# Layer normalisation of a small language-model tower: centred values kept in SBUF, variances of four pairs in one PSUM tile, deviations spread by row tiles

## The chip, the cores and the metric

One core of one Trainium2 chip runs the whole program in a single launch. The metric is the device time of that launch in microseconds (us), lower is better.

## The reference

The tower takes 32 sequences of 512 tokens, turns them into features of width 64 and passes them through four residual blocks. Each block first normalises its input without gain or bias:

```python
def _layernorm(x, axis=-1, eps=1e-05):
    m = jnp.mean(x, axis=axis, keepdims=True)
    v = jnp.var(x, axis=axis, keepdims=True)
    return (x - m) / jnp.sqrt(v + eps)

h = _L0_tok_ref(x, ...)                       # spectral tokenizer
h = h + _L0_attn_ref(_layernorm(h), ...)      # neighbourhood attention
h = h + _L0_ffn_ref(_layernorm(h), ...)       # mixture of experts, top 2 of 8
h = h + _L1_attn_ref(_layernorm(h), ...)      # decayed linear attention
h = h + _L1_ffn_ref(_layernorm(h), ...)       # soft mixture; its router takes the mean
                                              # of the normalised rows over the batch
```

## The kernel before

The residual stream `s.h` and the normalised values `s.z` live in SBUF for the whole program, as rows of 128 partitions by 512 columns in float32. One row is a pair of sequences: partitions 0 to 63 are the features of the first, 64 to 127 those of the second, columns are tokens. There are NP = 16 pairs. The program is a string of stages, each a block of its own with five instruction streams (TensorE, ScalarE, VectorE, GpSimd, SyncE) that meet at its end; only then does the next stage begin. `layer_norm` is such a stage and stands four times in the string, as ln0 to ln3, ahead of the four residual blocks. No stage prefetches anything for the next.

Inside `layer_norm`, for each pair: TensorE multiplies `s.h` by `center` (identity minus the mean over 64 features) into one of four PSUM tiles `cen` (L703). ScalarE squares it into SBUF, `sq` (L720). TensorE multiplies `sq` by `mean64`, a 128 by 128 matrix of two 64 by 64 blocks, so that every partition of `var` (one of four PSUM tiles) holds the variance of its own sequence (L708). ScalarE takes the logarithm of the variance plus eps (L725) and the exponential of minus half of it (L730), the reciprocal deviation `rstd`. VectorE multiplies `cen`, from PSUM, by `rstd` into `s.z` (L740). In ln3 GpSimd also adds every row of `s.z` to `s.feat` as it comes (L761); in ln0 it clears and fills two window buffers.

The order on each engine is written out by hand: `staggered` and `unrolled` take stages with a lead, and at step n each engine issues, in the order of the list, stage by stage, the work of pair n + lead. TensorE issues the variance of pair n + 2 and the centre of pair n + 4; ScalarE the root of n, the logarithm of n + 1, the squares of n + 3. `staggered` puts the middle of the work in a hardware loop of four pairs, `unrolled` writes all out. Engines wait for each other by counting semaphores; `done(n)` is the count at which pair n is finished, and a negative n is satisfied from the start.

Of the kernel before, what the change touches and what calls it, by code (L numbers as in the profile page):

```python
# [21 lines left out]
F32 = mybir.dt.float32  # L22
# [27 lines left out]
def window_start(t):  # L50
# [2 lines left out]

CONST_PARTS = [("ident", 128), ("dft", 4 * 2 * NF), ("shift", T), ("center", 128), ("mean64", 128), ("mean128", 128),
               ("decay", 128), ("chunk_q", 128), ("chunk_k", 1), ("winmask", 4 * WIN), ("headmask", HL), ("vmask", 18), ("rank", NE),
               ("pick", EP * 128), ("moe_b2", 2)]
CONST_AT = {}
# [8 lines left out]
def constants():  # L68
    c = {}
    c["ident"] = np.eye(128)  # L70
    block = np.kron(np.eye(2), np.full((D, D), 1.0 / D))
    c["center"] = np.eye(128) - block
    c["mean64"] = block
    c["mean128"] = np.full((128, 128), 1.0 / HID)
    t = np.arange(T)[:, None] * np.arange(NF)[None, :] % T * (2 * np.pi / T)
    dft = np.concatenate([np.cos(t), -np.sin(t)], 1)
    c["dft"] = dft.reshape(4, 128, 2 * NF).transpose(1, 0, 2).reshape(128, -1)

    step = np.float32(2.0 * np.pi / T)
    shift = (step * np.arange(T, dtype=np.float32)[None, :]) * np.arange(NF, dtype=np.float32)[:, None]  # L80
    shift = shift.astype(np.float64)
    c["shift"] = np.concatenate([np.cos(shift), np.sin(shift)] * 2, 0)
    k, q = np.arange(128)[:, None], np.arange(128)[None, :]
    c["decay"] = np.where(q >= k, np.power(float(np.float32(ALPHA)), np.maximum(q - k, 0)), 0.0) / np.sqrt(D)
    c["chunk_q"] = np.broadcast_to(np.power(float(np.float32(ALPHA)), q + 1) / np.sqrt(D), (128, 128))
    c["chunk_k"] = np.power(float(np.float32(ALPHA)), 127 - k)
    mask = np.full((4, QT, WIN), NEG)
    for kind, tile in enumerate((0, 1, 2, NT - 1)):
        for r in range(QT):
            first = min(max(tile * QT + r - KW // 2, 0), TG - KW) - window_start(tile)  # L90
            mask[kind, r, first:first + KW] = 0.0
    c["winmask"] = np.tile(mask.transpose(1, 0, 2).reshape(QT, -1), (4, 1))
    c["headmask"] = np.kron(np.ones((4, 1)), np.kron(np.eye(HL), np.ones((DH, 1))))
    v = np.zeros((128, 18))
    v[:WIN, 0:8] = v[WIN:2 * WIN, 8:16] = 1.0
    v[:WIN, 16] = v[WIN:2 * WIN, 17] = 1.0
    c["vmask"] = v
    c["rank"] = np.broadcast_to(np.arange(NE, 0, -1), (128, NE))
    pick = np.zeros((4, ROUTES, EP, 128))
    for e in range(NE):  # L100
        pick[:, [e, NE + e], e // 2, (e % 2) * 64:(e % 2) * 64 + 64] = 1.0
    c["pick"] = pick.reshape(128, -1)
    parts = np.zeros((4, ROUTES, 2))
    parts[:, 0:2 * NE, 0] = parts[:, 2 * NE:3 * NE, 1] = 1.0
    c["moe_b2"] = parts.reshape(128, 2)
    return np.ascontiguousarray(np.concatenate([c[n] for n, _ in CONST_PARTS], 1).astype(np.float32))

# [80 lines left out]
def const(s, name, rows=128):  # L188
    at, n = CONST_AT[name]
    return s.const[0:rows, at:at + n]  # L190
# [248 lines left out]
def done(n):  # L439

    return n + (1 + CREDITS)


def give_credits(eng, *semaphores):
    for sem in semaphores:
        eng.sem_inc(sem, CREDITS)  # L446


def row(t, n):

    return t[:, bass.ds(n, 1), :].rearrange("p a b -> p (a b)")
# [16 lines left out]
def staggered(eng, count, unroll, *stages):  # L468


    most = max(lead for lead, _ in stages)
    for n in range(-most, 0):
        for lead, stage in stages:
            if n + lead >= 0:
                stage(Step(0, n + lead, unroll))
    last = max(1, -(-most // unroll))
    turns = count // unroll - last
    with eng.Fori(0, turns) as turn:
        for k in range(unroll):
            for lead, stage in stages:  # L480
                stage(Step(turn, k + lead, unroll))
    for k in range(last * unroll):
        for lead, stage in stages:
            if k + lead < last * unroll:
                stage(Step(turns, k + lead, unroll))


def unrolled(count, unroll, *stages):


    most = max(lead for lead, _ in stages)
    for n in range(-most, count):
        for lead, stage in stages:
            if 0 <= n + lead < count:
                stage(Step((n + lead) // unroll, (n + lead) % unroll, unroll))
# [188 lines left out]
def layer_norm(nc, s, tag, features=False, windows=None):  # L684


    with ExitStack() as ctx:
        def sb(name):
            return [ctx.enter_context(nc.sbuf_tensor(f"{tag}_{name}{k}", [128, T], F32)) for k in range(4)]

        sq, ln, rstd = sb("sq"), sb("ln"), sb("rstd")
        cen, var = [[ctx.enter_context(nc.psum_tensor(f"{tag}_{x}{k}", [128, T], F32)) for k in range(4)] for x in ("cen", "var")]
        s_cen, s_sq, s_var, s_ln, s_rstd, s_z, s_feat = [ctx.enter_context(nc.semaphore(f"{tag}_s_{x}"))
                                                         for x in ("cen", "sq", "var", "ln", "rstd", "z", "feat")]
        block = ctx.enter_context(nc.Block())

        @block.tensor
        def _(te):
            give_credits(te, s_cen, s_var)

            def centre(at):
                te.wait_ge(s_z, done(at.n - 4))
                nc.tensor.matmul(cen[at.k][:], const(s, "center"), row(s.h, at.n), start=True, stop=True).then_inc(s_cen, 1)  # L703

            def variance(at):
                te.wait_ge(s_sq, done(at.n))
                te.wait_ge(s_ln, done(at.n - 4))
                nc.tensor.matmul(var[at.k][:], const(s, "mean64"), sq[at.k][:], start=True, stop=True).then_inc(s_var, 1)  # L708

            staggered(nc.tensor, NP, 4, (2, variance), (4, centre))  # L710

        @block.scalar
        def _(sc):
            sc.preload_act_table_set("natural_log_exp_and_others")
            give_credits(sc, s_sq, s_ln, s_rstd)

            def squares(at):
                sc.wait_ge(s_cen, done(at.n))
                sc.wait_ge(s_var, done(at.n - 4))
                nc.scalar.activation(sq[at.k][:], cen[at.k][:], ACT.Square).then_inc(s_sq, 1)  # L720

            def logarithm(at):
                sc.wait_ge(s_var, done(at.n))
                sc.wait_ge(s_rstd, done(at.n - 4))
                nc.scalar.activation(ln[at.k][:], var[at.k][:], ACT.Ln, bias=s.eps[:]).then_inc(s_ln, 1)  # L725

            def root(at):
                sc.wait_ge(s_ln, done(at.n))
                sc.wait_ge(s_z, done(at.n - 4))
                nc.scalar.activation(rstd[at.k][:], ln[at.k][:], ACT.Exp, scale=-0.5).then_inc(s_rstd, 1)  # L730

            staggered(nc.scalar, NP, 4, (0, root), (1, logarithm), (3, squares))

        @block.vector
        def _(ve):
            give_credits(ve, s_z)

            def normalise(at):
                ve.wait_ge(s_rstd, done(at.n))
                nc.vector.tensor_tensor(row(s.z, at.n), cen[at.k][:], rstd[at.k][:], ALU.mult).then_inc(s_z, 1)  # L740

            staggered(nc.vector, NP, 4, (0, normalise))

        @block.gpsimd
        def _(pool):
            if windows:
                for t in windows:
                    nc.gpsimd.memset(t[:], 0.0).then_inc(s_feat, 1)
                pool.wait_ge(s_feat, 2)
                for t in windows:  # L750
                    sums = t[:, :, :, :, 16:18].rearrange("p a b c d -> p (a b c) d")
                    nc.gpsimd.tensor_tensor(sums, sums, const(s, "vmask")[:, 16:18].unsqueeze(1).broadcast_to([128, 2 * NT * NH, 2]), ALU.add)\
                        .then_inc(s_feat, 1)
                pool.wait_ge(s_feat, 4)
            if features:
                give_credits(pool, s_feat)

                def add(at):
                    pool.wait_ge(s_z, done(at.n))
                    pool.wait_ge(s_feat, done(at.n - 1))  # L760
                    nc.gpsimd.tensor_tensor(s.feat[:], s.feat[:], row(s.z, at.n), ALU.add).then_inc(s_feat, 1)  # L761

                staggered(nc.gpsimd, NP, 4, (0, add))
# [897 lines left out]
```

## Time and profile before

| what | value |
|---|---|
| median of 3 runs | 1034.17 us |
| lowest, highest | 1033.28, 1040.14 us |
| the profiled execution, its own time | 1035.37 us |
| its span, first to last instruction | 1033.6 us |
| TensorE busy | 931.0 us, 90% |
| ScalarE busy | 596.1 us, 58% |
| VectorE busy | 581.5 us, 56% |
| GpSimd busy | 174.6 us, 17% |

The profile is of one execution. Its span leaves out 1.8 us of that execution's own time, and the own time is 1.2 us above the median of the runs. Busy time of TensorE is the union of its matmuls, whose ends are modelled; weight loads are counted apart (PEld). A float32 matmul appears as two weight loads and two matmul records.

### The profile page before, as it was taken

To read this page: it belongs to the slowest core of one execution; us is meant where nothing else is said; L and a number is where in the kernel's file an instruction comes from. 1 tells how busy PE (TensorE), PEld (TensorE's weight loads), DVE (VectorE), ACT (ScalarE), POOL (GpSimd) and SP (SyncE) were. 2 spreads that over 40 slices of the span, in tenths; PEclk is the share of its full clock that TensorE was granted. 3 is DMA by queue.
4 is the path that set the end of the run, shared out by engine and by line. 5 is a ranking of instruction groups with operands and counts; after the bars stand their busy time and mean duration, and the time that the engine had idled before them with its cause. 6 is when DMAs were issued, how large, how long until landed. Compare 5 with 4: busy or idle time off the path is not lost. (4 is left out here: it accounts for less than half of the span.)

```text
span 1033.6 us, 29479 instructions
## 1 busy us (share of the span) xinstructions
PE 931.0 (90%) x12388; PEld 449.2 (43%) x12388; DVE 581.5 (56%) x797; ACT 596.1 (58%) x822; POOL 174.6 (17%) x209
## 2 busy tenths in 40 slices
PE   3977969999999998937999999979999689999998
PEld 2331437767777675412222222347774422222222
DVE  3655237767777675366675755348873234444443
ACT  2998857777677775834444444742227445555553
POOL 1214121322313130061000000001114370000000
PEclk9998989999999999967999999989999899999999
DMA  2210000000000000000000000012110011111110
GB/s 54 28 28 1 0 1 5 4 4 4 4 4 5 4 4 3 1 1 1 1 1 1 1 1 1 1 42 53 42 32 1 0 36 56 43 42 42 41 42 31
DMA packets 27512, 17.15 MB, mean 17 GB/s; under 512 B 18753, under 2 KB 23010, under 8 KB 27394
## 3 DMA queue, kind: packets, MB, share of 16 engines
q1 hardware_dynamic: 26626, 14.16, 5.9%
q8 instruction: 97, 1.59, 0.6%
q10 hardware_dynamic: 768, 1.23, 0.3%
q14 instruction: 21, 0.17, 0.1%
HBM read 2.80 MB, written 4.19 MB: 7 GB/s over the span
## 5 line engine op out<-in xcount | busy, mean ns | idle before, releaser
L1585 DVE SCALAR_TENSOR_TENSOR se_a<-se_p,cols,z 128x1024 f32<-128x1024 f32 x64 | 82.2, 1284 | 119.1 <-PE se_p L1528 119.1
L1563 ACT ACTIVATE se_a<-se_p,cols 128x512 f32<-128x512 f32 x128 | 92.5, 773 | 79.9 <-PE se_p L1518 79.9
L1141 ACT ACTIVATE me_g<-me_p,cols 128x1024 f32<-128x1024 f32 x64 | 71.3, 1114 | 83.6 <-PE me_p L1095 83.6
L1232 DVE TENSOR_TENSOR me_gw<-me_pc,me_g 128x1024 f32<-128x1024 f32 x64 | 78.3, 1224 | 62.6 <-PE me_pc L1107 56.6
L991 DVE TENSOR_REDUCE na_rowmax<-na_ps 128x16 f32<-128x1024 f32 x64 | 78.0, 1218 | 60.9 <-PE na_ps L887 60.9
L801 POOL TENSOR_TENSOR z<-na_k,const 128x512 f32<-128x512 f32 x64 | 64.5, 1040 | 210.3 <-ACT na_k L940 210.3
L740 DVE TENSOR_TENSOR z<-ln_cen,ln_rstd 128x512 f32 (+1 forms) x64 | 44.2, 691 | 85.3 <-ACT ln_rstd L730 85.3
L994 DVE TENSOR_TENSOR na_e<-na_ps,na_rowmax 128x1024 f32<-128x1024 f32 x64 | 78.3, 1224 | 2.2
L703 PE MATMUL ln_cen<-h,const 128*128 (+1 forms) x128 | 69.7, 634 | 6.2 <-DVEq L446 6.2
L1518 PE MATMUL se_p<-z,f_w 64*64 64x512 f32 x256 | 70.5, 623 | 4.0 <-DMA se_zswap<-z 4.0
L896 PE MATMUL na_pt<-const,na_e 128*128 128x128 f32 x512 | 69.2, 278 | 3.3 <-ACT na_et L970 1.7
L1095 PE MATMUL me_p<-z,moe_w 64*64 64x512 f32 x512 | 70.7, 623 | 0.0
L970 ACT ACTIVATE na_et<-na_pt 128x1024 f32<-128x1024 f32 x64 | 65.4, 1023 | 8.7 <-PE na_pt L896 7.8
L1518 PE MATMUL se_p<-se_zswap,f_w 64*64 64x512 f32 x256 | 69.7, 623 | 0.0
L1538 PE MATMUL se_py<-se_a,f_wo 128*64 128x512 f32 x256 | 69.1, 618 | 0.4 <-DVE se_a L1585 0.4
L1117 PE MATMUL me_py<-me_gw,moe_w 128*64 128x512 f32 x256 | 69.0, 618 | 0.4 <-DVE me_gw L1232 0.4
L963 ACT ACTIVATE na_e<-na_e 128x1024 f32<-128x1024 f32 x64 | 67.4, 1054 | 1.5 <-DVE na_e L994 1.1
L1528 PE MATMUL se_p<-se_a,f_w 64*64 64x512 f32 x512 | 67.2, 595 | 1.1 <-DVE se_a L1585 1.1
L708 PE MATMUL ln_var<-ln_sq,const 128*128 128x512 f32 x128 | 65.8, 601 | 0.0
L896 PEld LDWEIGHTS na_pt<-const,na_e 128*128 128x128 f32 x512 | 56.2, 141 | 14.8 <-issue 12.0
L957 ACT ACTIVATE na_v<-na_pm 64x512 f32<-64x512 f32 x64 | 38.5, 602 | 29.0 <-PE na_pm L847 28.6
L913 PE MATMUL na_po<-na_v,na_et 128*32 128x18 f32 x4096 | 49.2, 187 | 4.4 <-issue 3.1
(222 smaller groups left out, 1539.1 us busy)
## 6 DMA issues: line engine op xcount, KB each, us to landing
da_zswap<-z SPq DMA_DIRECT2D x32, 128.0 KB, 2.3
se_zswap<-z SPq DMA_DIRECT2D x32, 128.0 KB, 2.4
out<-se_rows SPq DMA_DIRECT2D x16, 256.0 KB, 2.1
const<-in_const ACTq DMA_DIRECT2D x1, 720.5 KB, 5.0
f_w<-in_L_ffn_W SPq DMA_DIRECT2D x4, 128.0 KB
const<-in_const ACTq DMA_DIRECT2D x1, 448.0 KB, 3.9
moe_w<-in_L_ffn_w SPq DMA_DIRECT2D x2, 128.0 KB
raw<-in_L_ffn_b SPq DMA_DIRECT2D x12, 2.0 KB
```

The source lines that it names most:

```text
L703: nc.tensor.matmul(cen[at.k][:], const(s, "center"), row(s.h, at.n), start=True, stop=True).then_inc(s_cen, 1)
L896: mm = nc.tensor.transpose(p_t[:, c, :], e[b][:, 2 * c:2 * c + 2, :].rearrange("p h w -> p (h w)"), const(s, "ident"))
L991: nc.vector.tensor_reduce(rowmax[b][:], scored, AX, ALU.max).then_inc(s_max, 1)
L994: nc.vector.tensor_tensor(e[b][:], scored, rowmax[b][:].unsqueeze(2).broadcast_to([128, GROUPS, WIN]), ALU.subtract).then_inc(s_diff, 1)
L1095: mm = nc.tensor.matmul(p_1[half[e2], b, :], s.moe_w1[half[b], 2 * ep + e2, :], row(s.z, at.of(4))[half[b], :], start=True, stop=True, ski ...
L1117: mm = nc.tensor.matmul(p_y[slot][half[b], :], s.moe_w2[:, ep, :], gw[at.k % 2][:, b, :], start=False, stop=(ep == EP - 1), skip_group_che ...
L1141: nc.scalar.activation(g[at.k % 2][:], p_1[:], ACT.Gelu, bias=col(s, "moe_b1", ep)).then_inc(s_g, 1)
L1232: nc.vector.tensor_tensor(gw[at.k % 2][:], p_c[:], g[at.k % 2][:], ALU.mult).then_inc(s_gw, 1)
L1518: mm = nc.tensor.matmul(p_1[at.k % 2][half[b], e2, :], s.f1_w1[half[e2], 2 * ep + e2, :], z[half[e2], :], start=True, stop=True, skip_grou ...
L1538: mm = nc.tensor.matmul(p_y[half[b], :], s.f1_wo[:, ep, :], a2[at.k % 2][:, b, :], start=(ep == 0), stop=(ep == EP - 1), skip_group_check= ...
L1563: ins = nc.scalar.activation(a1[at.k % 2][:, e2, :], p_1[at.k % 2][:, e2, :], ACT.Relu, scale=col(s, "f1_g1", 2 * ep + e2), bias=col(s, "f ...
L1585: nc.vector.scalar_tensor_tensor(out=a2[at.k % 2][:], in0=p_2[:], scalar=col(s, "f1_be2", ep), in1=s.f1_w[:, ep, :].unsqueeze(1).broadcast ...
```

## The change

All of it is in `layer_norm` and in two constants.

- VectorE copies each `cen` tile to `s.z` (`move`) and later multiplies it there in place (`normalise`). ScalarE squares from `s.z`. `cen` has three tiles in place of four, and a centre matmul waits for the move of the pair three before it.
- `mean64` shrinks from 128 to 32 columns, of which two are not zero. The variances of four pairs go to the four 32-partition quarters of a single tile `var`, by four matmuls of 128 rows by 32 columns of the array.
- ScalarE takes one logarithm and one exponential for four pairs, the second in place on the first.
- TensorE spreads each quarter of `rstd` over 128 partitions with a new constant `select` (32 rows by 128 columns of the array), into one of four tiles `wide`. There is one set of `wide`.
- All three engines run `unrolled`, with leads of 9, 4 and 3 pairs on TensorE (centre, variance, spread), 7 and 4 on ScalarE (squares, deviations), 8 and 0 on VectorE (move, normalise). GpSimd's part is as it was.

```diff
-    c["mean64"] = block
+    c["mean64"] = np.kron(np.eye(2, 32), np.full((D, 1), 1.0 / D))
+    c["select"] = np.tile(np.kron(np.eye(32, 2), np.ones((1, D))), (4, 1))
...
-        sq, ln, rstd = sb("sq"), sb("ln"), sb("rstd")
-        cen, var = [[... [128, T], F32)) for k in range(4)] for x in ("cen", "var")]
+        sq, rstd = sb("sq", 8), sb("rstd", 2)
+        cen, var, wide = ps("cen", 3), ps("var", 1)[0], ps("wide", 4)
...
             def centre(at):
-                te.wait_ge(s_z, done(at.n - 4))
-                nc.tensor.matmul(cen[at.k][:], const(s, "center"), row(s.h, at.n), start=True, stop=True).then_inc(s_cen, 1)
+                te.wait_ge(s_moved, done(at.n - 3))
+                nc.tensor.matmul(cen[at.n % 3][:], const(s, "center"), row(s.h, at.n), start=True, stop=True).then_inc(s_cen, 1)
 
             def variance(at):
-                te.wait_ge(s_sq, done(at.n))
-                te.wait_ge(s_ln, done(at.n - 4))
-                nc.tensor.matmul(var[at.k][:], const(s, "mean64"), sq[at.k][:], start=True, stop=True).then_inc(s_var, 1)
-
-            staggered(nc.tensor, NP, 4, (2, variance), (4, centre))
+                if at.k == 3:
+                    te.wait_ge(s_sq, done(at.n))
+                    te.wait_ge(s_ln, done(at.of(4) - 1))
+                    for j in range(4):
+                        mm = nc.tensor.matmul(var[32 * j:32 * j + 32, :], const(s, "mean64"), sq[(at.n - 3 + j) % 8][:], start=True, stop=True,
+                                              skip_group_check=True)
+                    mm.then_inc(s_var, 1)
+
+            def spread(at):
+                if at.k == 3:
+                    q = at.of(4)
+                    te.wait_ge(s_rstd, done(q))
+                    te.wait_ge(s_z, done(4 * q - 1))
+                    for j in range(4):
+                        r = slice(32 * j, 32 * j + 32)
+                        mm = nc.tensor.matmul(wide[j][:], const(s, "select")[r, :], rstd[q % 2][r, :], start=True, stop=True, skip_group_check=True)
+                    mm.then_inc(s_wide, 1)
+
+            unrolled(NP, 4, (9, centre), (4, variance), (3, spread))
...
             def squares(at):
+                sc.wait_ge(s_moved, done(at.n))
+                sc.wait_ge(s_var, done((at.n - 8) // 4))
+                nc.scalar.activation(sq[at.n % 8][:], row(s.z, at.n), ACT.Square).then_inc(s_sq, 1)
+
+            def deviations(at):
+                if at.k == 3:
+                    q = at.of(4)
+                    sc.wait_ge(s_var, done(q))
+                    sc.wait_ge(s_wide, done(q - 2))
+                    nc.scalar.activation(rstd[q % 2][:], var[:], ACT.Ln, bias=s.eps[:]).then_inc(s_ln, 1)
+                    sc.wait_ge(s_ln, done(q))
+                    nc.scalar.activation(rstd[q % 2][:], rstd[q % 2][:], ACT.Exp, scale=-0.5).then_inc(s_rstd, 1)
+
+            unrolled(NP, 4, (7, squares), (4, deviations))
...
+            def move(at):
+                ve.wait_ge(s_cen, done(at.n))
+                nc.vector.tensor_copy(row(s.z, at.n), cen[at.n % 3][:]).then_inc(s_moved, 1)
 
             def normalise(at):
-                ve.wait_ge(s_rstd, done(at.n))
-                nc.vector.tensor_tensor(row(s.z, at.n), cen[at.k][:], rstd[at.k][:], ALU.mult).then_inc(s_z, 1)
-
-            staggered(nc.vector, NP, 4, (0, normalise))
+                ve.wait_ge(s_wide, done(at.of(4)))
+                ve.wait_ge(s_sq, done(at.n))
+                nc.vector.tensor_tensor(row(s.z, at.n), wide[at.k][:], row(s.z, at.n), ALU.mult).then_inc(s_z, 1)
+
+            unrolled(NP, 4, (8, move), (0, normalise))
```

## Rows read from the trace of the kernel before

**Rows 1.** The four layer_norm stages, ln0 to ln3: busy time per stretch.

```profile
core 0: us, PE busy (x) PEld busy (x) DVE busy (x) ACT busy (x) POOL busy (x), PEclk, DMA share, GB/s
103.60:135.70 32.10, 29.50 (x64) 12.51 (x64) 11.06 (x16) 28.22 (x49) 4.85 (x4) 0.95 0.00 0
...
779.80:812.00 32.20, 27.90 (x64) 11.85 (x64) 11.06 (x16) 28.19 (x49) 20.29 (x16) 0.98 0.00 1
```

**Rows 2.** Timeline of ln0, mid-stage: start us, duration us, engine, line.

```profile
112.27 1.02 PE L708 MATMUL ln_var<-ln_sq,const 128*128 128x512 f32 x2
...
113.12 1.02 PE L703 MATMUL ln_cen<-h,const 128*128 x2
...
113.98 1.02 PE L708 MATMUL ln_var<-ln_sq,const 128*128 128x512 f32 x2
...
114.18 0.60 ACT L720 ACTIVATE ln_sq<-ln_cen 128x512 f32<-128x512 f32 x1
...
114.68 0.62 ACT L730 ACTIVATE ln_rstd<-ln_ln 128x512 f32<-128x512 f32 x1
```

**Rows 3.** Timeline of ln1: its first centre, first variance, first normalise, last deviation.

```profile
414.72 3.59 PE L703 MATMUL ln_cen<-h,const 128*128 128x512 f32 x4 [1.41 <-DVEq L446]
...
418.14 1.02 PE L708 MATMUL ln_var<-ln_sq,const 128*128 128x512 f32 x2
...
421.32 0.69 DVE L740 TENSOR_TENSOR z<-ln_cen,ln_rstd 128x512 f32 x1 [7.22 <-ACT ln_rstd L730]
...
444.95 0.67 ACT L725 ACTIVATE ln_ln<-ln_var,eps 128x512 f32<-128x512 f32 x1
...
445.65 0.63 ACT L730 ACTIVATE ln_rstd<-ln_ln 128x512 f32<-128x512 f32 x1
446.31 0.69 DVE L740 TENSOR_TENSOR z<-ln_cen,ln_rstd 128x512 f32<-128x512 f32 x1 [0.55 <-ACT ln_rstd L730]
```

**Rows 4.** Timeline of ln3: first centre, last additions, last normalise, next stage.

```profile
779.81 1.95 PE L703 MATMUL ln_cen<-h,const 128*128 128x512 f32 x4 [1.35 <-DVEq L446]
...
807.85 4.08 POOL L761 TENSOR_TENSOR feat<-feat,z 128x512 f32<-128x512 f32 x3 [0.45 <-DVE z L740]
...
809.55 0.69 DVE L740 TENSOR_TENSOR z<-ln_cen,ln_rstd 128x512 f32<-128x512 f32 x1 [0.55 <-ACT ln_rstd L730]
...
812.27 2.04 PE L1424 MATMUL sr_p<-f_wr,feat 128*128 128x128 f32 x8 [4.57 <-PEq L687]
```

**Rows 5.** Timeline of the soft experts: three sets of tiled matmuls.

```profile
850.65 0.64 PE L1518 MATMUL se_p<-z,f_w 64*64 64x512 f32 x1
...
851.55 1.04 PE L1528 MATMUL se_p<-se_a,f_w 64*64 64x512 f32 x8
...
852.52 1.08 PE L1538 MATMUL se_py<-se_a,f_wo 128*64 128x512 f32 x4
...
853.53 0.64 PE L1518 MATMUL se_p<-z,f_w 64*64 64x512 f32 x1
```

**Rows 6.** Windows of L1072 alone (router, four 128*32 tiles), at full clock.

```profile
500.00:520.00 20.00, 1.07 (x8) 0.16 (x8) 1.00 0.00 1
```

**Rows 7.** Groups of matmuls by form: tiles of 32 rows.

```profile
L887 PE MATMUL na_ps<-z,na_q 32*32 32x256 f32 x2048 | 51.9, 390 | 0.2 <-issue 0.2
...
L1107 PE MATMUL me_pc<-me_ct,pick_r 32*128 32x512 f32 x128 | 32.1, 495 | 0.7 <-DVE me_gw L1232 0.4
```

**Rows 8.** Timeline of VectorE in the decayed attention: two reads of PSUM in a row.

```profile
689.33 0.69 DVE L1375 TENSOR_TENSOR da_v<-da_pv,a_bvk 128x512 f32<-128x512 f32 x1 [7.56 <-PE da_pv L1316]
...
689.94 0.74 DVE L1376 SCALAR_TENSOR_TENSOR da_kd<-da_pv,const,a_bvk 128x512 f32<-128x512 f32 x1
```

**Rows 9.** Copies on VectorE by form, from PSUM and from SBUF.

```profile
L1176 DVE COPY me_logits<-me_pr 128x256 f32<-128x256 f32 x4 | 1.7, 417 | 4.6 <-PE me_pr L1077 4.6
L1221 DVE COPY me_ctin<-me_high 128x256 f32<-128x256 f32 x4 | 1.2, 294 | 0.1
```

**Rows 10.** GpSimd additions by form, in the experts and in ln3.

```profile
L1059 POOL TENSOR_TENSOR h<-h,z 128x512 f32<-128x512 f32 x16 | 21.5, 1379 | 0.0
L761 POOL TENSOR_TENSOR feat<-feat,z 128x512 f32<-128x512 f32 x16 | 20.3, 1268 | 18.4 <-DVE z L740 18.1
```

More of the change, by code:

```diff
@@ L52, in window_start @@
     return min(max(t * QT - KW // 2, 0), TG - WIN)
-CONST_PARTS = [("ident", 128), ("dft", 4 * 2 * NF), ("shift", T), ("center", 128), ("mean64", 128), ("mean128", 128),
+CONST_PARTS = [("ident", 128), ("dft", 4 * 2 * NF), ("shift", T), ("center", 128), ("mean64", 32), ("select", 128), ("mean128", 128),
                ("decay", 128), ("chunk_q", 128), ("chunk_k", 1), ("winmask", 4 * WIN), ("headmask", HL), ("vmask", 18), ("rank", NE),
@@ L687, in layer_norm, with sb, ps @@
     with ExitStack() as ctx:
-        def sb(name):
-            return [ctx.enter_context(nc.sbuf_tensor(f"{tag}_{name}{k}", [128, T], F32)) for k in range(4)]
-        sq, ln, rstd = sb("sq"), sb("ln"), sb("rstd")
-        cen, var = [[ctx.enter_context(nc.psum_tensor(f"{tag}_{x}{k}", [128, T], F32)) for k in range(4)] for x in ("cen", "var")]
-        s_cen, s_sq, s_var, s_ln, s_rstd, s_z, s_feat = [ctx.enter_context(nc.semaphore(f"{tag}_s_{x}"))
-                                                         for x in ("cen", "sq", "var", "ln", "rstd", "z", "feat")]
+        def sb(name, n):
+            return [ctx.enter_context(nc.sbuf_tensor(f"{tag}_{name}{k}", [128, T], F32)) for k in range(n)]
+        def ps(name, n):
+            return [ctx.enter_context(nc.psum_tensor(f"{tag}_{name}{k}", [128, T], F32)) for k in range(n)]
+        sq, rstd = sb("sq", 8), sb("rstd", 2)
+        cen, var, wide = ps("cen", 3), ps("var", 1)[0], ps("wide", 4)
+        s_cen, s_sq, s_moved, s_var, s_ln, s_rstd, s_wide, s_z, s_feat = [ctx.enter_context(nc.semaphore(f"{tag}_s_{x}"))
+                                                                         for x in ("cen", "sq", "moved", "var", "ln", "rstd", "wide", "z", "feat")]
         block = ctx.enter_context(nc.Block())
@@ L698, in _ @@
         def _(te):
-            give_credits(te, s_cen, s_var)
+            give_credits(te, s_cen, s_var, s_wide)
             def centre(at):
-                te.wait_ge(s_z, done(at.n - 4))
-                nc.tensor.matmul(cen[at.k][:], const(s, "center"), row(s.h, at.n), start=True, stop=True).then_inc(s_cen, 1)
+                te.wait_ge(s_moved, done(at.n - 3))
+                nc.tensor.matmul(cen[at.n % 3][:], const(s, "center"), row(s.h, at.n), start=True, stop=True).then_inc(s_cen, 1)
             def variance(at):
-                te.wait_ge(s_sq, done(at.n))
-                te.wait_ge(s_ln, done(at.n - 4))
-                nc.tensor.matmul(var[at.k][:], const(s, "mean64"), sq[at.k][:], start=True, stop=True).then_inc(s_var, 1)
-            staggered(nc.tensor, NP, 4, (2, variance), (4, centre))
+                if at.k == 3:
[15 more added lines that the diff above has]
+            unrolled(NP, 4, (9, centre), (4, variance), (3, spread))
         @block.scalar
@@ L717, in squares @@
             def squares(at):
[L718 to L732, printed above, removed]
+                sc.wait_ge(s_moved, done(at.n))
[10 more added lines that the diff above has]
+            unrolled(NP, 4, (7, squares), (4, deviations))
         @block.vector
         def _(ve):
-            give_credits(ve, s_z)
+            give_credits(ve, s_moved, s_z)
+            def move(at):
+                ve.wait_ge(s_cen, done(at.n))
+                nc.vector.tensor_copy(row(s.z, at.n), cen[at.n % 3][:]).then_inc(s_moved, 1)
             def normalise(at):
-                ve.wait_ge(s_rstd, done(at.n))
-                nc.vector.tensor_tensor(row(s.z, at.n), cen[at.k][:], rstd[at.k][:], ALU.mult).then_inc(s_z, 1)
-            staggered(nc.vector, NP, 4, (0, normalise))
+                ve.wait_ge(s_wide, done(at.of(4)))
+                ve.wait_ge(s_sq, done(at.n))
+                nc.vector.tensor_tensor(row(s.z, at.n), wide[at.k][:], row(s.z, at.n), ALU.mult).then_inc(s_z, 1)
+            unrolled(NP, 4, (8, move), (0, normalise))
         @block.gpsimd
```

## The prediction

> **What bounds the kernel now.** I read the page's busy times first (TensorE 90%), then the busy time of the four normalisation stages by windows, then their timelines, because stages don't overlap and only these four change. Each stage is 32.1 to 32.3 us long and TensorE is busy in 28 to 29.5 us of it, ScalarE in 28.2, VectorE in 11.1 [rows 1]. The timeline shows what sets the pace: centre, variance and centre start 0.85 and 0.86 us apart [rows 2], so a pair costs TensorE 2 x 0.858 = 1.716 us and four pairs 6.86 us; nothing in between is idle. ScalarE, three operations a pair, starts them 0.5 us apart at the closest (square to exponential, 114.18 to 114.68 [rows 2]) and keeps up, just. ln1 runs from its first centre at 414.72 to the end of its last normalise at 446.31 + 0.69 = 447.00: 32.28 us. Its first two centres take until 418.14, 1.71 us each, twice 0.858: that is the clock at 1.2 in place of 2.4 GHz after the idle of the stage's start [rows 3]. ln3 starts at the full clock and its z is ready at 810.24, but what ends it is GpSimd: three additions in 4.08 us, 1.36 us from one to the next, up to 811.93, and the router's first matmul starts at 812.27 [rows 4]. So ln3 is 32.12 us long, and its end hangs on additions of which 16 need 21.8 us.
>
> **The price of a set of tiles.** The trace has no set like the new two, but near ones. In the soft experts a set of four 64*64 matmuls is followed after 0.90 us by another of the same form, and sets followed by another form take 0.97 and 1.01 us [rows 5]. So a set of tiles that covers the array costs 0.90 us against 0.858 for one full matmul, and a change of form some 0.12 us more. The router's set of four 128*32 tiles is the form of the new variance: 1.07 us from start to the end of its results [rows 6], in line with 1.04 and 1.08 in rows 5. The Trainium skill ("TensorEngine Tiling (Array Packing)", Key Properties) says that changing the tiling mode drains TensorE; the trace agrees, and prices the drain at about 0.12 us. I take 1.02 us for variance and spread alike, plus 0.12 where a centre stands before one.
>
> The spread is the less certain. Its four tiles of 32 rows each write all 128 partitions of a bank of their own, in float32. For it speaks L887: 32 float32 matmuls of 256 columns in tiles of 32*32, all four row groups, in 51.9 / 32 = 1.62 us a step, where row groups taken one after another would need 8 x 0.43 = 3.4 us [rows 7]. L1107 has two 32*128 tiles side by side, 32.1 / 64 = 0.50 us for both [rows 7]. Bounds: 0.90 us (rows 5) and 4 x 0.858 = 3.43 us, no overlap; I take the low end, since both nearest rows overlap. The Trainium skill ("TensorE: Matmul & The Clock Gate", Measured speedup vs the span model) gives a speedup of 3.07 for four row tiles of 512 columns; by that the set would take 3.43 / 3.07 = 1.12 us (an estimate from that page), and the sum would be about 1.5 us longer.
>
> **The other parts.** Two PSUM-reading operations on VectorE start 0.61 us apart, and the first takes 0.69 [rows 8]. A copy of 256 columns from PSUM takes 0.417 us and from SBUF 0.294 [rows 9], so the move has no short form; between 0.417 and twice that for 512 columns, I take the 0.69 of an operation of that size in rows 8, 0.61 from start to start and 0.74 until a waiter goes on. Eight of them, for four pairs, are 4.9 us: under what TensorE needs, however VectorE is now close behind. ScalarE falls from twelve operations to six for four pairs and is free. Logarithm to exponential is 0.70 us and exponential to the waiting engine 0.66 [rows 3]. `const` grows by 32 columns, loaded stages before: nothing. The written-out loops replace hardware loops; I cost that at nothing, as the other stages are written out and TensorE runs without gaps in them [rows 5].
>
> **What replaces the bound.** By count, four pairs now take TensorE 4 x 0.858 + 2 x 1.02 + 0.12 = 5.6 us, 1.3 less than 6.86. But its queue is in order: variance of group g, one centre, spread of group g, three centres. From the start of a variance to the start of its spread lie 1.07 (matmuls) + 0.08 (hand-over) + 0.70 + 0.66 = 2.51 us, and the one centre fills only up to 1.02 + 0.86 = 1.88. TensorE stands 0.6 us in each group, with centres queued behind the wait. The period is 0.12 + 2.51 + 1.02 + 3 x 0.858 = 6.22 us, a gain of 0.64, not 1.3. VectorE's loop (seven operations from one group's first normalise, 6 x 0.61 + 0.74, then the next spread 1.15) is 5.55 us and fits below.
>
> Head: nine centres must go out before the first variance, where before it followed the second. In ln1 the first two end at 3.42, the ninth at 9.43; variance 9.55, spread 12.06, first normalise 1.15 later at 13.21 (before: 6.60 [rows 3]). Then the second group's normalise at 19.43, and the last centre ends at 21.02. The third group: variance 21.14, but its logarithm stands behind the square of pair 14, whose move starts at 21.26 and ends by 22.0, and 0.5 after that square's start it starts, at 22.5; spread 23.86, normalise 25.01. The fourth: variance 24.88, but the single set of `wide` is free only when pair 11 is done, 25.01 + 3 x 0.61 + 0.74 = 27.6; spread 27.6, four normalises from 28.75, the end at 31.27. Against 32.28 ln1 gains 1.0 us; ln0 and ln2 start as cold, so 3.0 us for the three.
>
> ln3 is warm, so everything is 1.70 us earlier: normalises of the four groups begin at 11.51, 17.73, 23.31 and 27.05. The first addition starts at 12.25 and each group's four take 5.44 us: 12.25 to 17.69, 18.47 to 23.91, 24.05 to 29.49, then without a pause to 34.93. Before it was 32.12: a loss of 2.8 us, since GpSimd gets its first row 5 us later than before and has no speed to make it up. If additions are slowed by VectorE's doubled work (1.38 us in place of 1.27, as L1059 in the experts [rows 10]), 16 x 0.11 = 1.8 us more.
>
> **Sum.** -3.0 + 2.8 = -0.2 us against the profiled execution's own 1035.37, so 1035.2; that run was 1.2 above the median, so 1034.0. A kernel whose runs spread from 1033 to 1040 can't tell less than 1% from no change. The forecast's own range is 1029 to 1039: 0.12 us up or down for each of 16 groups' two sets, and the additions' 1.8.
>
> **Rivals.**
> - *The spread's tiles go two at a time.* Each set then takes 2 x 0.858 + 0.12 = 1.84, 0.82 more, and all of it lies on the path: four times in ln0 to ln2, 9.8 us, and in ln3 the last group's additions begin about 2.5 us later. 1034.0 + 12.3 = 1046, slower by 1.2%; at full serial order some 1070. It decides once a set costs over 1.65 us. Against it: L887 and L1107. For it: no row has four full-width float32 outputs at once. 0.10 (with the serial end).
> - *The count decides.* If the spread found its deviations ready, TensorE would set the pace and ln0 to ln2 would end with it: 1.7 + 16 x 0.858 + 8 x 1.02, then 1.15 + 3 x 0.61 + 0.69, is 27.3 us, 4.0 less than above for each of three stages: 1034.0 - 12 = 1022, faster by 1.2%. For it: TensorE is what bounds these stages. Against it: the order of the queue and 1.36 us of ScalarE in series. 0.10.
> - *VectorE takes over.* If its operations start 0.75 us apart and not 0.61, its loop is 6 x 0.75 + 0.88 (0.14 longer as well) + 1.15 = 6.5 us, over 6.22, and the tails grow by 0.6 us: 1034.0 + 4 = 1038. 0.08, inside the range. The Trainium skill names this outcome ("TensorEngine Tiling (Array Packing)", PSUM Bottleneck: the copy out of PSUM may become the bottleneck after tiling); here rows 8 speak against it.
> - *The change doesn't do what it says*: float32 tiles don't overlap at all, the serial end above.
>
> The forecast has 0.72, with VectorE's case 0.80. Range 1025 to 1043, which leaves out 0.2 at the two ends. Faster by over 1%: 0.12; within 1%: 0.75; slower by over 1%: 0.13, the last with a little for slow hand-overs that I haven't found.
>
> **What the changed profile would show.** Right: the variance and spread sets 1.0 to 1.1 us each; TensorE idle about 0.6 us before each spread, released by ScalarE; first normalises near 13.2 us after the first centre (11.5 in ln3), groups 6.2 us apart; ln0 to ln2 about 31.3 us long; GpSimd's additions without a gap from the second half of ln3 on, ending 35 us after the first centre. Wrong: a spread of 1.6 us or more; normalises under 6 us apart; a third clock-bound centre in the head; additions that end with the last normalise.

## The result, and the profile after

The changed kernel takes 1039.72 us (median of 19 runs, 1036.72 to 1047.66) against 1035.26 for the kernel before in as many runs: ratio 1.005, 95% interval 1.0034 to 1.0066. It is slower by about 5 us (3.5 to 6.8 by the interval). The forecast was 1034.0, no change, in a range of 1025 to 1043: the time lies in the range, but the loss is real and was not forecast. The profiled execution took 1038.47, its span is 1036.7 us.

Stage by stage, from the first matmul of one to the first of the next, read from the timelines of both traces (us):

```
                      before   after
up to ln0              103.6   105.5   not touched by the change
ln0                     33.7    31.7
neighbourhood attn.    277.4   276.9
ln1                     33.5    31.2
experts                201.5   201.5
ln2                     35.5    35.2
decayed attention       94.6    94.7
ln3                     32.5    36.8
router                  18.0    19.2
soft experts           203.2   204.2
```

Before anything is read into ln0 and ln1, the clock has to be taken out. After, they happened to start at 2.4 GHz and ln2 at 1.2; before, all three started at 1.2. Windows of the four changed stages (columns as in [rows 1]):

```profile
105.40:135.50 30.10, 23.31 (x96) 7.57 (x96) 20.35 (x32) 15.57 (x25) 4.73 (x4) 0.99 0.00 0
414.00:444.00 30.00, 23.30 (x96) 7.53 (x96) 20.35 (x32) 15.50 (x25) 0.00 (x0) 0.96 0.00 1
646.60:678.40 31.80, 25.00 (x96) 8.21 (x96) 20.34 (x32) 15.59 (x25) 0.00 (x0) 0.93 0.00 1
776.50:813.00 36.50, 23.30 (x96) 7.57 (x96) 20.35 (x32) 15.56 (x25) 20.30 (x16) 0.92 0.00 0
```

TensorE's busy time fell from some 28 to 29.5 us to 23.3 or 25.0 and ScalarE's from 28.2 to 15.6, as the change meant. VectorE's rose from 11.1 to 20.4. The stages did not shorten with TensorE. From first centre to last normalise they take 29.98 us from a warm clock (ln0, ln1, ln3) and 31.67 from a cold one (ln2); before, 30.43 (ln3) and 32.04 (ln0, ln2). Like for like, such a stage gains 0.4 us. ln1 before was the longest, 32.28 from a cold clock; it took 30.75 from a warm one where the old stage ran in a later kernel (e2), and the changed one took 31.61 from a cold clock in another (e3). So ln1 gains 0.7 us, and ln0 to ln2 together gain 1.5.

TensorE in ln3, after, shows why (timeline: start us, duration us; in brackets the idle before it and what ended it):

```profile
776.55 7.96 PE L707 MATMUL ln_cen<-h,const 128*128 128x512 f32 x18 [1.50 <-DVEq L447]
784.44 1.06 PE L714 MATMUL ln_var<-ln_sq,const 128*32 128x512 f32 x8
785.44 1.12 PE L707 MATMUL ln_cen<-h,const 128*128 128x512 f32 x2
786.98 1.14 PE L725 MATMUL ln_wide<-ln_rstd,const 32*128 32x512 f32 x8 [0.42 <-ACT ln_rstd L747]
788.05 2.84 PE L707 MATMUL ln_cen<-h,const 128*128 128x512 f32 x6
790.82 1.06 PE L714 MATMUL ln_var<-ln_sq,const 128*32 128x512 f32 x8
791.82 1.12 PE L707 MATMUL ln_cen<-h,const 128*128 128x512 f32 x2
793.36 1.14 PE L725 MATMUL ln_wide<-ln_rstd,const 32*128 32x512 f32 x8 [0.42 <-ACT ln_rstd L747]
...
799.01 1.14 PE L725 MATMUL ln_wide<-ln_rstd,const 32*128 32x512 f32 x8 [1.60 <-ACT ln_rstd L747]
800.08 1.06 PE L714 MATMUL ln_var<-ln_sq,const 128*32 128x512 f32 x8
802.85 1.14 PE L725 MATMUL ln_wide<-ln_rstd,const 32*128 32x512 f32 x8 [1.70 <-DVE z L762]
813.31 2.05 PE L1446 MATMUL sr_p<-f_wr,feat 128*128 128x128 f32 x8 [9.32 <-PEq L688]
```

The sets cost what was assumed: variance to centre 1.00 us (784.44 to 785.44), spread to centre 1.07 (786.98 to 788.05). From one spread to the next is 6.38 us (786.98 to 793.36), with a wait for the deviations in each, and the last two spreads wait 1.60 and 1.70 us. The first spread is 10.43 us after the first centre. And after the last one TensorE idles 9.32 us, where it was 4.57 [rows 4]. GpSimd works in that gap:

```profile
789.14 1.27 POOL L783 TENSOR_TENSOR feat<-feat,z 128x512 f32<-128x512 f32 x1 [19.34 <-DVE z L762]
790.67 1.28 POOL L783 TENSOR_TENSOR feat<-feat,z 128x512 f32<-128x512 f32 x1 [0.26 <-POOL feat L783]
...
795.52 1.28 POOL L783 TENSOR_TENSOR feat<-feat,z 128x512 f32<-128x512 f32 x1 [0.53 <-DVE z L762]
797.05 1.27 POOL L783 TENSOR_TENSOR feat<-feat,z 128x512 f32<-128x512 f32 x1 [0.24 <-POOL feat L783]
...
804.56 1.26 POOL L783 TENSOR_TENSOR feat<-feat,z 128x512 f32<-128x512 f32 x1 [0.24 <-POOL feat L783]
806.07 6.89 POOL L783 TENSOR_TENSOR feat<-feat,z 128x512 f32<-128x512 f32 x5 [0.24 <-DVE z L762]
```

The reader is to see three things. The first addition starts 12.59 us into the stage. The fifth (795.52) waits 0.53 us for its row, the first of the second group; from it on the chain runs without such a gap to 812.96. And in the middle an addition follows another after some 1.51 us, while the last four, which stand behind the hardware loop, follow the one before after (6.89 - 1.27) / 4 = 1.41. The last z was ready at 804.05 + 2.48 = 806.53, 6.4 us before the stage could end.

The router behind it, before and after (windows, same columns; the eighth figure is the granted clock):

```profile
812.30:830.30 18.00, 10.83 (x48) 8.28 (x48) 2.54 (x8) 4.44 (x7) 2.96 (x3) 0.76 0.09 20
```

```profile
813.30:832.40 19.10, 11.98 (x48) 9.44 (x48) 2.54 (x8) 4.48 (x7) 2.89 (x3) 0.68 0.09 19
```

The same 48 matmuls keep TensorE busy 1.15 us longer at a mean clock of 0.68 in place of 0.76. That isn't the mark of the changed ln3: the kernel of e10 below has the old ln3, with the old idle of 4.57 us ahead of the router, and its router is longer still.

```profile
810.20:829.70 19.50, 12.14 (x49) 9.58 (x49) 2.54 (x8) 4.43 (x7) 3.15 (x3) 0.68 0.10 21
```

Its soft experts take 204.2 us, as in the changed kernel. Over all profiles the router and soft experts together take 221.3 to 223.8 us with the old ln3 and 221.7 to 223.4 with a changed one that has its additions and no filler.

### The profile page after: what moved, and what is told of

The parts are those of the page before. It is cut to its first block and busy times, and to the rows that moved or that the text cites. A ratio compares the mean times of both kernels' runs of the same rounds, so it can differ in the third digit from the quotient of the medians.

```text
span 1036.7 us, 29247 instructions
## 1 busy us (share of the span) xinstructions
PE 912.6 (88%) x12516; PEld 433.0 (42%) x12516; DVE 618.6 (60%) x861; ACT 546.5 (53%) x726; POOL 174.8 (17%) x209
## 3 DMA queue, kind: packets, MB, share of 16 engines
q8 instruction: 99, 1.62, 0.7%
## 5 line engine op out<-in xcount | busy, mean ns | idle before, releaser
L707 PE MATMUL ln_cen<-h,const 128*128 128x512 f32 x128 | 61.8, 622 | 6.8 <-DVEq L447 6.8
L762 DVE TENSOR_TENSOR z<-ln_wide,z 128x512 f32<-128x512 f32 x64 | 41.8, 684 | 28.7 <-PE ln_wide L725 28.7
L738 ACT ACTIVATE ln_sq<-z 128x512 f32<-128x512 f32 x64 | 39.3, 627 | 28.3 <-DVE z L757 28.3
L757 DVE COPY z<-ln_cen 128x512 f32<-128x512 f32 x64 | 44.0, 687 | 14.8 <-PE ln_cen L707 14.8
```

## The experiments

All times are in runs beside the kernel before; a ratio has its 95% interval behind it. In the mixed kernels the old stage stands in the program under another name, with its own 128-column block of means as a further constant.

**Which stage loses.** Two mixed kernels, the changed stage in ln0 to ln2 alone and in ln3 alone; the first was run again later.

```diff
-        layer_norm(nc, s, "ln3", features=True)
+        layer_norm_old(nc, s, "ln3", features=True)
```

> ln0, ln1 and ln2 as in the changed kernel, ln3 as before. Theory A (the loss lies in ln3 alone, where GpSimd's chain of additions starts late): from the first centre to the last normalise ln0 to ln2 take about 31.7 us from a cold clock or 30.0 from a warm one, 0.4 to 0.6 less than before each; in all 1 to 2 us faster than before, ratio 0.998 to 0.999. Theory B (the new stage costs a little everywhere, in its waits, its written-out code or the clock behind it, and each of the four stages carries a quarter): slower by 3 to 4 us, ratio 1.003 to 1.004.

Measured: 1038.28 us, ratio 1.0012 (0.9995 to 1.0029). It falls between the two: Theory A's 0.998 to 0.999 lies below the interval, Theory B's 1.003 to 1.004 above it.

> Only ln3 as in the changed kernel, ln0 to ln2 as before. Theory A: ln3 is 4.3 us longer (36.8 in place of 32.5 from its first centre to the router's first matmul) and the router behind it up to 1 us longer, at a lower clock: 5 to 6 us slower than before, ratio 1.005 to 1.006. Theory B: 1 to 1.5 us slower, ratio 1.001 to 1.0015.

Measured: 1041.95 us, ratio 1.0067 (1.0041 to 1.0093); ln3 to the router's first matmul 36.7 us, the router 19.8. Theory B's 1.0015 is out: the changed stage in ln3 alone costs what the whole change costs.

> The mixed kernel once more (ln0 to ln2 changed, ln3 as before), to narrow its time. By the lengths of the stages (31.1 us on the mean of five profiles, before 31.3 on the mean of two) it should be 0.5 to 1 us faster than before, ratio 0.9992; by its first timing 1.0012. If it is 1.001 or more again, changed ln0 to ln2 cost some 2 us in stages that the change doesn't touch.

Measured: 1035.9 us, ratio 1.0006 (0.9987 to 1.0026). So ln0 to ln2 together are worth nothing that can be measured, and Theory B's 1.003 is out here too. The 0.9992 that was expected lies in this interval and not in e1's. The gain of 1.5 us that the lengths show like for like (cold start against cold, warm against warm) would be 0.9985; it lies outside both intervals, of this one by little. So some 2 us seem to be lost in a place that the lengths of these stages don't show, and where stays open. The profiles don't point at one: the neighbourhood attention takes 277.4 to 279.8 us behind an old ln0 and 276.9 to 283.5 behind a changed one.

**What holds ln3.** First the hardware loop taken from the additions, then the additions themselves left out, so that the router sees zeros.

```diff
-                staggered(nc.gpsimd, NP, 4, (0, add))
+                unrolled(NP, 4, (0, add))
```

> The changed kernel with GpSimd's additions written out in place of a hardware loop. Theory A, with the step between additions in a loop (1.51 us) longer than outside one (1.37): 12 additions gain 0.14 each, ln3 is 1.7 us shorter, 3 to 3.5 us slower than before in all, ratio 1.003. Rival: 1.51 is what an addition takes beside VectorE's doubled work, and the last ones are faster only since VectorE is done; then the step stays 1.51 and nothing changes (ratio 1.005).

Measured: 1041.07 us, ratio 1.0052 (1.0035 to 1.0069), not told apart from the changed kernel. The trace is clearer than the time: one profile row now holds twelve additions.

```profile
792.50 5.54 POOL L783 TENSOR_TENSOR feat<-feat,z 128x512 f32<-128x512 f32 x4 [19.16 <-DVE z L762]
798.88 16.78 POOL L783 TENSOR_TENSOR feat<-feat,z 128x512 f32<-128x512 f32 x12 [0.83 <-DVE z L762]
```

Their step is (16.78 - 1.27) / 11 = 1.41 us beside the same VectorE work, so the rival is out: 1.51 belongs to the loop, not to VectorE. The stage is 35.9 us, 0.85 shorter and not 1.7. The step fell by 0.10 us and not 0.14, and what the first group gains is lost again, since GpSimd then waits longer for the second group's rows (0.83 us idle at 798.88, 0.53 before).

> The changed kernel without the additions of the normalised rows in ln3 (the router sees zeros). Theory A: ln3 ends with its last normalise, 6.4 us earlier, and the router starts after a shorter idle of TensorE; 2 us faster than before, ratio 0.998, and 6 to 7.5 us faster than the changed kernel. Theory B: the additions matter by what they overhang in the kernel before, 1.7 us; then 3 us slower than before remain, ratio 1.003.

The kernel leaves out the sum over the batch of the last normalised rows. Measured: 1034.66 us, ratio 0.9993 (0.9978 to 1.0008), by the ratios some 6 us faster than the changed kernel (5.1 by the medians); ln3 is 30.3 us, 6.5 shorter, the router 18.5. The loss is gone with the additions. The interval holds Theory A's 0.998 and excludes 1.003. But the lengths alone, 1.5 us less in ln0 to ln2 and 2.2 less in ln3, would give 0.9964, which is outside too: here again 1.4 to 4.5 us are spent somewhere else.

**Which wait holds the stage itself.** The order of the queues alone is changed: each spread one centre later, each move one pair earlier. The two are tested together.

```diff
-            unrolled(NP, 4, (9, centre), (4, variance), (3, spread))
+            unrolled(NP, 4, (9, centre), (4, variance), (2, spread))
...
-            unrolled(NP, 4, (8, move), (0, normalise))
+            unrolled(NP, 4, (9, move), (0, normalise))
```

> The changed kernel with each spread one centre later in TensorE's queue and each move one pair earlier in VectorE's. If the wait for the deviations, with centres queued behind it, sets the period of 6.38 us for four pairs, TensorE then has no wait left there and the period is 5.75; the first normalise comes 0.2 later, so ln0 to ln2 are 1.0 us shorter each (29.0 from a warm clock) and ln3, which its additions end, 0.2 longer: 2.8 us faster than the changed kernel, ratio to before 1.002. If VectorE or the hand-overs set it, the period stays near 6.4 and the time that of the changed kernel.

Measured: 1041.09 us, ratio 1.0064 (1.0045 to 1.0083). The period is now 5.9 us (first normalises of two groups 429.33 and 435.23), so it was the order of the queues, with the wait for the deviations in it, that set 6.38. A warm stage (ln1) takes 29.25 us where 29.0 was expected, 0.7 less than 29.98, and ln3 stays at 36.7. The time shows none of it, and in this profile there is little to show: ln0 is even 0.9 us longer than a cold stage of the changed kernel (32.55 against 31.67), and ln2, from a warm clock, takes 30.66, 0.7 more than 29.98. ln0's tail on TensorE:

```profile
127.96 1.14 PE L725 MATMUL ln_wide<-ln_rstd,const 32*128 32x512 f32 x8 [1.84 <-DVE z L762]
129.03 1.93 PE L714 MATMUL ln_var<-ln_sq,const 128*32 128x512 f32 x8
132.43 2.09 PE L725 MATMUL ln_wide<-ln_rstd,const 32*128 32x512 f32 x8 [1.47 <-ACT ln_rstd L747]
```

The last variance and spread take 1.93 and 2.09 us in place of 1.06 and 1.14: the granted clock fell to 1.2 GHz after the wait of 1.84, inside the stage. In ln2 the same happened, with 1.77 and 2.09 us after a wait of 1.84:

```profile
671.55 1.77 PE L714 MATMUL ln_var<-ln_sq,const 128*32 128x512 f32 x8
674.77 2.09 PE L725 MATMUL ln_wide<-ln_rstd,const 32*128 32x512 f32 x8 [1.45 <-ACT ln_rstd L747]
```

So in two of these three stages, in this profile, the low clock ate the gain of the new order.

Then the head too: seven centres ahead of the first variance in place of nine.

```diff
-            unrolled(NP, 4, (9, centre), (4, variance), (2, spread))
+            unrolled(NP, 4, (7, centre), (4, variance), (2, spread))
...
-            unrolled(NP, 4, (7, squares), (4, deviations))
+            unrolled(NP, 4, (6, squares), (4, deviations))
...
-            unrolled(NP, 4, (9, move), (0, normalise))
+            unrolled(NP, 4, (7, move), (0, normalise))
```

> As the last, and with seven centres ahead of the first variance in place of nine. First normalise 10.2 us after the first centre from a warm clock (changed kernel: 11.6), ln0 to ln2 28.0 long to the last normalise (29.98), ln3's additions end 1.6 us earlier since they start so much earlier: 7.5 us faster than the changed kernel, ratio to before 0.998. If the additions in ln3 don't follow their start, that part is nothing and the ratio 0.9995.

Measured: 1032.61 us, ratio 0.9988 (0.9961 to 1.0015). The first normalise comes at 10.29 us and the stage takes 28.15, as expected within 0.2. In ln3:

```profile
780.95 1.28 POOL L783 TENSOR_TENSOR feat<-feat,z 128x512 f32<-128x512 f32 x1 [18.00 <-DVE z L762]
...
786.97 1.27 POOL L783 TENSOR_TENSOR feat<-feat,z 128x512 f32<-128x512 f32 x1 [0.19 <-POOL feat L783]
...
797.51 6.89 POOL L783 TENSOR_TENSOR feat<-feat,z 128x512 f32<-128x512 f32 x5 [0.25 <-POOL feat L783]
```

The stage's first centre is at 769.70. The additions start at 11.25 us and end at 34.70, against 12.59 and 36.41: 1.34 us earlier at one end, 1.7 at the other. The fifth addition (786.97) now waits for the fourth and not for its row, so the gap ahead of the second group is gone; it starts at 17.27 us where it was 18.97, and that is all of the 1.7. In e5 the first addition starts 0.38 us later than in the changed kernel, the fifth at 18.98, and the additions end at 36.38 as before. So the end of ln3 follows the point from which GpSimd has no gap any more, even though the rows of the last group are there at 28.15.

**A version that beats both.** The short-head stages in ln0 to ln2, and the old one in ln3.

> The last one's ln0 to ln2 and ln3 as before: faster than before by 3 x (32.0 - 29.7) = 7 us by the stages' lengths, ratio 0.9935. If new stages ahead of the attention and the experts cost some 1 us each in the stages behind them (as the second timing of mixed stages, 1.0012 where the lengths gave 0.9985, would have it), 0.996.

Measured: 1027.6 us, ratio 0.9944 (0.9915 to 0.9974). It is faster than both. TensorE in its ln1 shows what bounds it now:

```profile
421.16 1.98 PE L790 MATMUL ln_cen<-h,const 128*128 128x512 f32 x4
423.08 1.14 PE L808 MATMUL ln_wide<-ln_rstd,const 32*128 32x512 f32 x8
424.15 1.98 PE L790 MATMUL ln_cen<-h,const 128*128 128x512 f32 x4
426.06 1.06 PE L797 MATMUL ln_var<-ln_sq,const 128*32 128x512 f32 x8
427.06 1.98 PE L790 MATMUL ln_cen<-h,const 128*128 128x512 f32 x4
428.97 1.14 PE L808 MATMUL ln_wide<-ln_rstd,const 32*128 32x512 f32 x8
...
434.62 1.14 PE L808 MATMUL ln_wide<-ln_rstd,const 32*128 32x512 f32 x8 [0.54 <-ACT ln_rstd L830]
...
438.46 1.14 PE L808 MATMUL ln_wide<-ln_rstd,const 32*128 32x512 f32 x8 [1.62 <-DVE z L845]
```

From the first centre on TensorE has no wait until the third spread. Four centres and two sets take it 5.89 us (423.08 to 428.97), and that is the period: in the middle of the stage TensorE's own work is the bound again. Only the tail waits, 0.54 us for the deviations and 1.62 for the single set of `wide` tiles. VectorE has idle time in every group:

```profile
424.29 0.69 DVE L845 TENSOR_TENSOR z<-ln_wide,z 128x512 f32<-128x512 f32 x1 [1.27 <-PE ln_wide L808]
424.89 0.68 DVE L840 COPY z<-ln_cen 128x512 f32<-128x512 f32 x1
...
430.18 0.69 DVE L845 TENSOR_TENSOR z<-ln_wide,z 128x512 f32<-128x512 f32 x1 [1.02 <-PE ln_wide L808]
...
435.83 2.48 DVE L845 TENSOR_TENSOR z<-ln_wide,z 128x512 f32<-128x512 f32 x4 [0.77 <-PE ln_wide L808]
439.66 2.48 DVE L845 TENSOR_TENSOR z<-ln_wide,z 128x512 f32<-128x512 f32 x4 [1.34 <-PE ln_wide L808]
```

Its operations follow each other after 0.60 us, a group after 5.89, and the single set of `wide` tiles leaves it idle for 1.34 us between the last two groups.

**Is the clock behind the stages worth anything?** Centre matmuls that nobody reads were put where TensorE idles: nine after ln3's last spread in the changed kernel; one before and three after the last spread of ln0 to ln2 in the version above; two in the tails of ln0 to ln2 in the kernel before.

```diff
+            if features:
+                te.wait_ge(s_moved, done(NP - 1))
+                for n in range(9):
+                    nc.tensor.matmul(cen[n % 3][:], const(s, "center"), row(s.h, n), start=True, stop=True)
```

> The changed kernel with nine more centre matmuls, whose results nobody reads, behind ln3's last spread, while GpSimd adds. If the idle of 9.3 us lowers TensorE's clock in the router (12.3 us of its 19.2 at 1.2 GHz, before 8.5 of 18.0), it now runs at 2.4 GHz: router stage 16.5 to 17.5 us, 2 us less, ratio to before 1.003. If the clock there doesn't matter, 19 us still and 1.005.

Measured: 1039.5 us, ratio 1.0054 (1.0035 to 1.0073). The idle ahead of the router falls to 1.39 us, and its window is

```profile
815.50:833.10 17.60, 10.54 (x48) 8.08 (x48) 2.54 (x8) 4.46 (x7) 2.86 (x3) 0.81 0.09 21
```

1.5 us shorter in this profile at a clock of 0.81, and the soft experts take 203.3, but the time doesn't show it: the ratio is that of the changed kernel.

> The short-head stages for ln0 to ln2, ln3 as before, and centre matmuls that nobody reads in the tails of ln0 to ln2: one ahead of the last spread, three behind it. If what TensorE idles in these tails (1.6 and 4.2 us) is paid behind them at 1.2 GHz (first matmul of the attention 2.05 us in place of 1.28, of the experts 1.93 in place of 1.49), each of the three stages behind is 0.5 to 1.5 us shorter: 2 to 4 us faster than the same without fillers, ratio to before 0.991 to 0.992. If the clock of those few matmuls doesn't matter, 0.9944 again.

Measured: 1028.77 us, ratio 0.9939 (0.992 to 0.9959), against 0.9944 without fillers: the same, and not the 0.991 to 0.992 of the first theory.

> The kernel before with two centre matmuls that nobody reads in the tails of ln0 to ln2, where TensorE idles 3.8 us to the next stage. If a warm start of the stages behind is worth 0.5 to 1.5 us each, 0.997 to 0.998; if not, 1.000.

Measured: 1033.47 us, ratio 0.9984 (0.9964 to 1.0004), not told from no change, nor from the 0.997 to 0.998 of a gain. In the first two cases filling the idle was worth nothing that could be seen; in the third it was worth 1.7 us or nothing, and the interval reaches to 3.7.

## Why the prediction was wrong

The mechanism was read rightly, the sizes were not, and the two that decide were both off the same way. The sum was -3.0 + 2.8 = -0.2; like for like the traces show -1.5 + 4.3 = 2.8. What lies between these 2.8 us and the measured 5.2 no run explains.

```
ln3 (warm), us after first centre   predicted   measured
first normalise, group 1              11.51      11.64
                 group 2              17.73      18.02
                 group 3              23.31      23.67
                 group 4              27.05      27.50
last normalise ends                   29.57      29.98
first addition                        12.25      12.59
last addition ends                    34.93      36.41
```

- *What bounds the kernel*: right. The pace of 1.716 us a pair is gone, and ln3's end hangs on the additions, as e4 (without them 30.3 us) and e6 (started 1.34 earlier, ended 1.7 earlier) show.
- *The price of a set of tiles*: right. 1.00 us for the variance and 1.07 for the spread, to the next centre, against 1.02 for both. Four row tiles of full-width float32 output do overlap; the rival with tiles two at a time lay far above. The 1.12 us that the prediction estimated from the Trainium skill ("TensorE: Matmul & The Clock Gate", Measured speedup vs the span model) lay 0.05 above the measured 1.07. The change of form ahead of the variance costs 0.20 us and not 0.12 (788.05 to 790.82 is 2.77, three centres are 2.57); ahead of the spread it isn't seen, since the spread waited anyway. One of the two rows for the overlap, L1107, was weaker than it was taken for: its constant `pick_r` is F32R in the kernel and a matmul of it leaves one record, where a float32 one leaves two.
- *The other parts*: right. The move is 0.69 us long, VectorE's operations start 0.60 us apart; VectorE did not take over. The larger `const` shows nothing: up to ln0 the profiles take 103.0 to 105.5 us, the two of the old form 103.6 and 104.8.
- *What replaces the bound*: right in kind, 6.38 us and not 6.22. Moving the spread behind one more centre, with the moves one pair earlier, took the wait away and brought 5.9.
- *The gain in ln0 to ln2, "ln1 gains 1.0 us; ln0 and ln2 start as cold, so 3.0 us for the three"*: twice too large; it is 0.7 in ln1 and 0.4 in the other two, 1.5 in all. Some 1.1 us of the miss is a walk that comes out 0.3 to 0.4 us longer in each stage (31.67 and 31.61 for 31.27), the rest is the base: ln1's 32.28 was taken for all three, where ln0 and ln2 had 32.04. That ln0 and ln1 started warm in the changed kernel's profile is no part of the gain: e1, e3 and e4 have them cold. The mixed kernels, at 1.0012 and 1.0006, see not even 1.5 us.
- *The loss in ln3, "three additions in 4.08 us, 1.36 us from one to the next", "16 need 21.8 us"*: the step that failed, together with the gain above. The chain of additions was the right path, with a step that was too short. The row of [rows 4] holds three additions in 4.08 us, and the prediction divided by three. Three additions have two steps and a last duration: (4.08 - 1.27) / 2 = 1.41. And those three stand behind the hardware loop; inside it a step is 1.51, which the trace of before hides, since there rows come only every 1.72 us. The loss in ln3 was forecast at 2.8 us and measured at 4.3 (36.41 against 32.12). Of the 1.5 us between, 1.0 is the step: from the second group's first addition to the end the prediction has 16.46 us (18.47 to 34.93), the trace 17.44 (18.97 to 36.41), and seven steps of 1.51, four of 1.41 and a last addition of 1.27 make 17.5. The other 0.5 is that the second group's rows come later. The estimate of a further 1.8 us from slower additions made room for such a miss, with a wrong cause: VectorE doesn't slow them (1.27 us each as before, 1.41 apart when written out). The words "5 us later than before" for GpSimd's first row are a slip: by the prediction's own figures it is 6.6 (13.21 against 6.60), and 6.6 was measured (12.59 against 6.02); the sum doesn't use them.
- *Behind ln3*: the sum has nothing there. In the changed kernel's profile the router took 1.1 us and the soft experts 0.9 longer, at a lower clock, and the wait of TensorE ahead of them had doubled. But e7, e9 and e10, with the old ln3 and the old wait, have routers of 18.9 to 19.5 us and soft experts of 204.3; and the filler in e8 took 1.5 us back in the profile but not in the time. So these 2 us differ from profile to profile and are not shown to come from the change.
- *The rivals*: "the count decides" was rightly given little for this queue. It is what holds in the middle of a stage of the short-head version, whose order leaves TensorE no wait there: 5.89 us for four pairs, where the count had 5.6.

What doesn't close: -1.5 + 4.3 is 2.8 us, and the measured ratio is 5.2 (3.5 to 6.8). To add the 2 us behind ln3 would fit the number by luck, since kernels with the old ln3 show them too. The same 2 us or so are missing in e1 and e10 (0.9985 by the lengths, 1.0012 and 1.0006 measured) and in e4 (0.9964 against 0.9993). The mixed kernels' ratios add to 1.0073 to 1.0079, 2 to 3 us more than the change as a whole; the intervals allow it. The clock differs from run to run as well, in ways that no term of the sum held: in e1 the granted clock was 0.50 for the first 5.1 us of ln1, which took 32.5 us where 31.6 is what it took in e3.

## What to carry to other kernels

Cutting an engine's work by batching delays the first result. Whoever consumes the results one by one at nearly the pace of production can't make up for it: here a chain of 16 additions, 24 us long without waits in a stage that was 32, turned a first row that came 6.6 us later into an end 4.3 us later. Before batching, look for the serial consumer on the slowest engine and give it the old order, or shorten the head first. After batching, the queue's order is where the gain lies: shorter leads (the four that e6 changed) took 1.8 us off each stage that the batching itself had shortened by 0.4 to 0.7.

When a merged row of a trace gives n operations in a span, the step is (span - one duration) / (n - 1), and a step that is read outside a hardware loop doesn't hold inside one.

## What the runs showed of the hardware

- GpSimd: an addition of 128x512 float32 is 1.27 us long, follows another it depends on after 1.41 us in written-out code and after 1.51 in the hardware loop (e3 against the changed kernel).
- TensorE: four 32*128 tiles of 512 columns in float32, each into a tile of its own, 1.07 us from start to the next form; four 128*32 tiles 1.00; one full matmul 0.858.
- The granted clock can fall inside a stage: in e5, after a wait of 1.84 us in TensorE's queue, the last two sets of ln0 took 1.93 and 2.09 us in place of 1.06 and 1.14, those of ln2 1.77 and 2.09. In ln1 and ln3 of the same program, with the same order, the same sets kept 1.06 or 1.07 and 1.14.
